# A fused attention and feed-forward kernel on one core: context sums copied whole and put together by DMA, a batch's last contexts in the next one's first step, row statistics and weight loads in pieces

## The reference

```python
x = x + _layernorm(attention(_layernorm(x), Wq, bq, Wk, bk, Wv, bv, Wo, bo))   # 32 heads of 16
x = x + _layernorm(ffn(_layernorm(x), gate_w, up_w, down_w, scales))           # 512 -> 1536 -> 512
# attention: softmax(q k^T / 4) v per head; ffn: down(silu(gate(x)) * up(x)),
# where each weight is first rounded to float8 (e4m3) and widened again
```

## Time and profile before

| | us |
|---|---|
| median of three runs (lowest, highest) | 1712.83 (1712.39, 1716.59) |
| the profiled execution's own time | 1714.72 |
| its span, first to last instruction | 1712.9 |
| PE busy | 1585.2 (93%) |
| DVE busy | 1191.8 (70%) |
| ACT busy | 908.0 (53%) |
| POOL busy | 619.7 (36%) |

### The profile page before, as it was taken

The page is one execution under the profiler, slowest core; times in us unless marked ns, Lnnn a source line. Parts: engine busy times, 40 slices in busy tenths (PEclk is TensorE's granted clock), DMA queues, the critical chain, the costliest instruction groups (busy, mean ns, idle before and its releaser), DMA issues.

```text
span 1712.9 us, 22893 instructions
## 1 busy us (share of the span) xinstructions
PE 1585.2 (93%) x8266; PEld 728.8 (43%) x8266; DVE 1191.8 (70%) x2200; ACT 908.0 (53%) x1624; POOL 619.7 (36%) x504
## 2 busy tenths in 40 slices
PE   4899999999999999999999999879999999999996
PEld 3433333333334334333333433215555555555553
DVE  6698898898888888888888888764254353353433
ACT  3177676666766767767767766672222222222221
POOL 4124343533633542542443352143332232232331
PEclk9799999999999999999999999979999999999998
DMA  3412212312211312321221121510201201201110
GB/s 115 102 37 72 52 45 71 88 50 65 79 56 50 97 35 60 91 55 51 84 73 49 46 81 41 164 56 19 87 25 50 74 25 49 75 25 50 50 50 25
DMA packets 81740, 105.63 MB, mean 62 GB/s; under 512 B 16214, under 2 KB 46934, under 8 KB 81624
## 3 DMA queue, kind: packets, MB, share of 16 engines
q1 hardware_dynamic: 81628, 104.17, 20.8%
HBM read 52.71 MB, written 21.50 MB: 43 GB/s over the span
## 4 chain that ended last, share of the span: by engine, by line
PE 61%; DVE 24%; ACT 8%; issue 5%; DMA 1%; POOL 1%; SPq 1%; POOLq 0%; ACTq 0%; DVEq 0%
PE ring L1371 19%; PE side L1001 13%; DVE maxima L832 11%; PE down_sums L1385 10%; PE contexts L1076 8%; PE scores L1063 6%; PE maxima_scores L1040 4%; ACT probs L741 3%; DVE channel_shift_bits L971 2%; DVE channel_shift_bits L969 1%; DVE denominators L857 1%; DVE qkT L816 1%; DVE stats_in L787 1%; DVE y L823 1%; DVE ctx_raw L862 1%
## 5 line engine op out<-in xcount | busy, mean ns | idle before, releaser
L832 DVE TENSOR_REDUCE maxima<-maxima_scores 128x1 f32<-128x512 f32 x1024 | 655.5, 679 | 92.7 <-PE maxima_scores L1040 87.4
L741 ACT ACTIVATE probs<-scores 128x512 f32<-128x512 f32 x1024 | 549.4, 601 | 283.8 <-PE scores L1063 283.1
L1040 PE MATMUL maxima_scores<-k_stack,q_stack 64*128 64x512 f16 x1024 | 340.2, 390 | 47.2 <-DVE maxima L832 46.7
L1063 PE MATMUL scores<-q_stack,k_stack 64*128 64x512 f16 x1024 | 326.8, 390 | 14.2 <-ACT probs L741 8.1
L1076 PE MATMUL contexts<-probs,v_around_ones 128*32 128x512 f32 x2048 | 278.7, 616 | 8.4 <-ACT denominators L685 3.5
L1321 DVE SCALAR_TENSOR_TENSOR fuse<-ring,up_scale,gate 128x512 f32<-128x512 f32 x96 | 72.0, 750 | 292.9 <-PE ring L1371 284.2
L1235 POOL TENSOR_TENSOR fuse_low<-fuse,fuse_high 128x512 fp32r<-128x512 f32 x96 | 137.8, 1436 | 372.7 <-ACT fuse_high L1257 372.7
L1257 ACT CAST fuse_high<-fuse 128x512 fp32r<-128x512 f32 x96 | 59.4, 619 | 291.9 <-PE down_sums L1385 270.0
L1063 PEld LDWEIGHTS scores<-q_stack,k_stack 64*128 64x128 f16 x1024 | 65.5, 94 | 339.6 <-ACT probs L741 183.2
L1385 PE MATMUL down_sums<-down_q,fuse_high 128*128 128x512 f32 x384 | 168.0, 437 | 1.1 <-issue 0.8
L1371 PE MATMUL ring<-xT_high_ffn,gate_q 128*128 128x512 f16 x384 | 146.6, 382 | 7.4 <-DVE xT_low_ffn L1294 5.9
(11 more groups left out here) (201 smaller groups left out, 2409.4 us busy)
## 6 DMA issues: line engine op xcount, KB each, us to landing
q_stack<-qkT SPq DMA_DIRECT2D x192, 64.0 KB, 2.0
k_stack<-qkT SPq DMA_DIRECT2D x192, 64.0 KB, 2.0
x_rows<-in_L_attn_hidden_states SPq DMA_DIRECT2D x8, 1024.0 KB, 5.3
x_residual<-in_L_attn_hidden_states SPq DMA_DIRECT2D x32, 256.0 KB, 2.9
middle_rows<-y SPq DMA_DIRECT2D x32, 256.0 KB, 3.3
x_rows_ffn<-middle_rows SPq DMA_DIRECT2D x8, 1024.0 KB, 5.6
x_residual_ffn<-middle_rows SPq DMA_DIRECT2D x8, 1024.0 KB, 7.9
out_rows<-y_ffn SPq DMA_DIRECT2D x32, 256.0 KB, 2.2
```

The source lines that it names most:

```text
L741: act.activation(probs[:, n % 2, j, :], work[(b * (GH * STEPS) + GH * n + j) % RING][:], ACT.Exp, scale=float(D) ** -0.5).then_inc(p_full, 1)
L832: dve.tensor_reduce(maxima[:, g % 2, at:at + 1], bank[:], AX.X, ALU.max).then_inc(rot_free, 1)
L1040: mm = pe.matmul(bank[:], q_st[half, s, qc * P:qc * P + P], k_st[half, s, :], start=True, stop=True)
L1063: mm = pe.matmul(work[i % RING][:], k_st[half, s, c * P:c * P + P], q_st[half, s, :], start=True, stop=True)
```

## The change

- **Context sums.** ACT copies the bank whole: after the even group to `ctx_raw` (one operation for two), after the odd group to a new tile `ctx_odd_groups`. DVE's two masked additions and its shuffle are gone. SP puts the halves together with DMAs of 16 partitions by 512: four for the even denominators (`denominators_even`, at n = 5, 13, 21, 29), and four for the odd denominators and four for the odd contexts (`contexts_together`, at n = 9, 17, 25 and at n = 1 of the next batch). ACT's `invert` now waits for those DMAs, POOL's `normalise` too.
- **Seam.** `contexts(b, 31)` moves from the end of the batch into step 0 of the next, between score 1 and score 2.
- **Order within steps.** ACT's `invert` stands inside the step, its logarithm behind exponential 1, its exponential behind exponential 3 (steps 2, 10, 20, 26), and `refine` behind exponential 1 of the step after. POOL's last reciprocal and `normalise` of a batch move from steps 1 and 2 of the next to 2 and 3. The transposes of the next batch's rows move from the end of steps 12 to 15 to the head of steps 13 to 16. The weight jobs move to other steps. `aggregate` is cut in two (three sums, then four more operations) in steps 3 and 4, 18 and 19; statistics of the next batch's rows are in steps 0 and 2 and no longer in 1 and 2. ACT's normalisation of the output rows is in steps 20 to 23.
- **FFN weights.** The last batch loads the scales at n = 14, gate and up weights in four pieces each at n = 15 to 22, the down weights in four pieces at n = 23 to 26; DVE widens three blocks each at the end of steps 28 to 31.

```diff
...
@@ -250,3 +259,3 @@
     MAXIMA = NH * T
-    XT0 = 12
+    XT0 = 13
@@ -273,3 +282,3 @@
         if XT0 <= n < XT0 + T and b < B - 1:
-            out.append((("x", n - XT0), b + 1))
+            out.insert(0, (("x", n - XT0), b + 1))
         if n >= STEPS - T and b == B - 1:
@@ -335,3 +344,3 @@
     MAGIC_AT, SUM_AT, BIG_AT, ROUND_AT, STORE_AT = (
-        (2, 7, 12, 22, 27), (3, 8, 13, 23, 28), (4, 9, 14, 24, 29), (5, 11, 15, 25, 30), (6, 12, 16, 26, 31))
+        (6, 10, 14, 20, 26), (7, 11, 15, 23, 29), (8, 12, 16, 24, 30), (9, 13, 18, 25, 31), (10, 14, 19, 26, 31))
     gate_w, up_w, down_w = ffn_weights
...
@@ -433,2 +443,22 @@
+        def denominators_even(k):
+            slot = k % O % 2
+            sp.wait_ge(c0_out, k + 1)
+            if k > 1:
+                sp.wait_ge(c_l, k - 1)
+            for j in range(GH):
+                lo = 2 * D * j
+                sp.dma_start(den[lo:lo + D, slot, :], ctx_raw[lo + D:lo + 2 * D, slot, :]).then_inc(den_even, 16)
+
+        def contexts_together(k):
+            slot = k % O % 2
+            sp.wait_ge(c1_out, k + 1)
+            for j in range(GH):
+                lo = 2 * D * j
+                sp.dma_start(den[lo + D:lo + 2 * D, slot, :], ctx_odd[lo:lo + D, :]).then_inc(den_odd, 16)
+            sp.wait_ge(den_even, (k + 1) * GH * 16)
+            for j in range(GH):
+                lo = 2 * D * j
+                sp.dma_start(ctx_raw[lo + D:lo + 2 * D, slot, :], ctx_odd[lo + D:lo + 2 * D, :]).then_inc(ctx_in, 16)
+
         fill(0, 0)
...
@@ -490,3 +522,10 @@
                     sp.dma_start(ffn.ds_rows[:], down_s.partition_broadcast(P)).then_inc(ffn.s_in, 16)
-                    sp.dma_start(ffn.down_in[:], down_d.rearrange("(f p) h -> p f h", p=P)).then_inc(ffn.w_in["down"], 16)
+                if last and 15 <= n < 15 + 2 * KC:
+                    name, c = ("gate", "up")[(n - 15) // KC], (n - 15) % KC
+                    rows, dst = ((gate_d, ffn.gate_q), (up_d, ffn.up_q))[(n - 15) // KC]
+                    sp.dma_start(dst[:, c, :], rows[c * P:c * P + P, :]).then_inc(ffn.w_in[name], 16)
+                if last and 23 <= n < 23 + DOWN_PARTS:
+                    part = ffn.F // DOWN_PARTS
+                    blocks = slice((n - 23) * part, (n - 23) * part + part)
+                    sp.dma_start(ffn.down_in[:, blocks, :], down_d.rearrange("(f p) h -> p f h", p=P)[:, blocks, :]).then_inc(ffn.w_in["down"], 16)
                 if n == 18 and b + 2 < B:
...
@@ -586,5 +627,5 @@
             for n in range(STEPS):
-                if n == 1 and b:
-                    times_reciprocal(b * O - 1, O - 1)
                 if n == 2 and b:
+                    times_reciprocal(b * O - 1, O - 1)
+                if n == 3 and b:
                     normalise(b * O - 1, O - 1, None)
...
@@ -683,4 +724,10 @@
                 act.wait_ge(c_l, b * O + o - 1)
-            act.mul(ctx_raw[:, o % 2, :], cps[:], half_mask[:, 0:1]).then_inc(c0_out, 1)
-            act.mul(den[:, o % 2, :], cps[:], half_mask[:, 1:2]).then_inc(c0_out, 1)
+            act.copy(ctx_raw[:, o % 2, :], cps[:]).then_inc(c0_out, 1)
+
+        def contexts_odd(k):
+            act.wait_ge(pv_done, PV0 + (2 * k + 2) * T)
+            if k > 0:
+                act.wait_ge(ctx_in, k * GH * 16)
+                act.wait_ge(den_odd, k * GH * 16)
+            act.copy(ctx_odd[:], cps[:]).then_inc(c1_out, 1)
@@ -688,7 +735,9 @@
-            act.wait_ge(den_sh, k + 1)
+            act.wait_ge(den_even, (k + 1) * GH * 16)
+            act.wait_ge(den_odd, (k + 1) * GH * 16)
             if k > 0:
                 act.wait_ge(c_l, k)
-
             act.activation(rec[:], den[:, o % 2, :], ACT.Ln).then_inc(den_ln, 1)
+
+        def invert_back(k):
             act.wait_ge(den_ln, k + 1)
...
@@ -725,14 +773,8 @@
                 before = side_end(b, n - 1)
+                if XT0 <= n < XT0 + T and not last:
+                    turned_high(b + 1, n - XT0)
                 if before:
                     side_high(before[1], before[0], side_at[before])
-                if n == 1 and b:
-                    invert(b * O - 1, O - 1)
-                if n == 2 and b:
-                    refine(b * O - 1, O - 1)
-                if n in (10, 20, 26):
-                    o = (10, 20, 26).index(n)
-                    invert(b * O + o, o)
-                if n in (11, 21, 28 if last else 27):
-                    o = n // 8 - 1
-                    refine(b * O + o, o)
+                inverted = {2: b * O - 1, 10: b * O, 20: b * O + 1, 26: b * O + 2}.get(n, -1)
+                refined = {3: b * O - 1, 11: b * O, 21: b * O + 1, 28 if last else 27: b * O + 2}.get(n, -1)
                 act.wait_ge(pv_done, PV0 + b * STEPS + n - 1)
@@ -741,10 +783,16 @@
                     act.activation(probs[:, n % 2, j, :], work[(b * (GH * STEPS) + GH * n + j) % RING][:], ACT.Exp, scale=float(D) ** -0.5).then_inc(p_full, 1)
+                    if j == 1 and inverted >= 0:
+                        invert(inverted, inverted % O)
+                    if j == 1 and refined >= 0:
+                        refine(refined, refined % O)
+                    if j == 3 and inverted >= 0:
+                        invert_back(inverted)
+                if n % 8 == 0 and b * O + n // 8:
+                    contexts_odd(b * O + n // 8 - 1)
                 if n % 8 == 4:
                     contexts_even(b, n // 8)
-                if XT0 <= n < XT0 + T and not last:
-                    turned_high(b + 1, n - XT0)
                 if n in (6, 7, 8, 9) and not last:
                     normalise("in", x_rows, xn_ready, b + 1, n - 6)
-                if n in (18, 19, 21, 22) and b:
-                    normalise("out", y, yn_ready, b - 1, (18, 19, 21, 22).index(n))
+                if 20 <= n < 20 + T and b:
+                    normalise("out", y, yn_ready, b - 1, n - 20)
                 j = job_at(BIG_AT, b, n)
...
@@ -852,17 +901,2 @@
-        def denominators_odd(b, o):
-            k = b * O + o
-            dve.wait_ge(pv_done, PV0 + b * STEPS + (2 * o + 2) * T)
-            dve.wait_ge(c0_out, (k + 1) * 2)
-            dve.scalar_tensor_tensor(den[:, o % 2, :], cps[:], half_mask[:, 0:1], den[:, o % 2, :], ALU.mult, ALU.add).then_inc(c1_out, 1)
-
-        def contexts_odd(b, o):
-            k = b * O + o
-            dve.wait_ge(c1_out, ODD0 + k * 2 + 1)
-            dve.scalar_tensor_tensor(ctx_raw[:, o % 2, :], cps[:], half_mask[:, 1:2], ctx_raw[:, o % 2, :], ALU.mult, ALU.add).then_inc(c1_out, 1)
-
-
-        def shuffle(o):
-            dve.stream_shuffle(den[:, o % 2, :], den[:, o % 2, :], [(i + D) % 32 for i in range(32)]).then_inc(den_sh, 1)
-
         def channel_factors():
@@ -932,6 +966,2 @@
                     first_rows()
-                if last and n == 24:
-                    dve.wait_ge(ffn.w_in["down"], 16)
-                    for f in range(ffn.F):
-                        dve.tensor_copy(ffn.down_q[:, f, :], ffn.down_in[:, f, :]).then_inc(ffn.down_ready, 1)
                 if last and n == 27:
@@ -941,4 +971,8 @@
                                           ffn.norms["in"]["rstd"][:, t:t + 1], ALU.subtract, ALU.mult).then_inc(ffn.xn_ready, 1)
-                for k, (item, of) in enumerate(items):
+                k = -1
+                for item, of in items:
                     reduce_maxima(of, item)
+                    if item[0] == "x":
+                        continue
+                    k += 1
                     if k == 0 and before:
...
@@ -953,12 +987,11 @@
                         stats("in", x_rows, t)
-                    if n == 3 and k == 1 and not last:
-                        moments("in", b + 1)
-                    if n == 18 and k == 1 and b:
-                        moments("out", b - 1)
-                    if n % 8 == 0 and n and k == 1:
-                        denominators_odd(b, n // 8 - 1)
-                    if n % 8 == 0 and n and k == 2:
-                        contexts_odd(b, n // 8 - 1)
-                    if n % 8 == 1 and n > 1 and k == 0:
-                        shuffle(n // 8 - 1)
+                    if n in (3, 4) and k == 1 and not last:
+                        moments("in", b + 1, ((sums, spreads)[n - 3],))
+                    if n in (18, 19) and k == 1 and b:
+                        moments("out", b - 1, ((sums, spreads)[n - 18],))
+                if last and n >= STEPS - DOWN_PARTS:
+                    part, i = ffn.F // DOWN_PARTS, n - STEPS + DOWN_PARTS
+                    dve.wait_ge(ffn.w_in["down"], DOWN_PARTS * 16)
+                    for f in range(i * part, (i + 1) * part):
+                        dve.tensor_copy(ffn.down_q[:, f, :], ffn.down_in[:, f, :]).then_inc(ffn.down_ready, 1)
                 j = job_at(MAGIC_AT, b, n)
...
@@ -1123,2 +1156,5 @@
                 what, i, lo, hi, later = side_step(b, n)
+                if items and items[0][0][0] == "x":
+                    rot_item(items[0][1], items[0][0])
```

(5 more changed lines are left out.)

## The result

The changed kernel takes 1630.34 us (three runs, 1627.21 to 1630.97) against 1712.83: a ratio of 0.9507, 95% interval [0.9479, 0.9535]. In a later comparison it took 1627.9 us, ratio 0.9499 [0.9486, 0.9512]. Forecast were 1634 us and a range of 1606 to 1672. The profiled execution has a span of 1629.0 us against 1712.9: 83.9 less, of which the six middle batches give 70.3 (136.73 to 125.02 in the mean), the first 7.9, the last 11.5; the tail behind the last contexts takes 5.6 more, the start 0.2.

The account below looks back on a forecast made before the run. PE bounds the kernel at 3.67 us a step and DVE interrupts it. Six middle batches -67, first batch -5, last -9, tail +2.2 sum to -78.8 us: 1712.8 to 1634 us, range 1606 to 1672.

Parts of the forecast that it names:

- Seam: Step 31 and the next step 0: PE no longer stands until ACT has made step 31's four exponentials, 10.3 to 7.5, -2.8 us.
- Context sums: DVE and ACT lose operations per pair; counted beyond the seam only in steps 8 to 11, 16.5 to 15.5, -1.0 us.
- 1 and 2: Steps 1 and 2 of a middle batch, now without a weight job: 8.5 to 7.5, -1.0 us.
- 17 to 20: Steps 17 to 20, where aggregate's seven operations, the shuffle and the inversion are taken apart: 16.95 to 15.1, -1.8 us.
- 26 to 28: Steps 26 to 28, where the weight job at n = 27 no longer falls in POOL's normalise: 12.4 to 11.3, -1.1 us.
- 22 and 23: Steps 22 and 23, where the weight job at n = 22 no longer falls in POOL's normalise: 8.7 to 7.4, -1.3 us.
- Steps 3 to 5: Up to three DVE waits for POOL's normalise in step 4 (L65, L67 above 1 us), or by another reading one: -1.2 us.
- 12 to 16: Row transposes ahead of their step: 22.9 to 21.4, -1.5 us; step 13 stays near 4.95 because of ACT's load.
- Step 21: ACT has four operations, 2.75 us, between steps 20 and 21, so score 3 waits: 4.4 to 4.95, +0.55 us.
- New DMAs: 48 per batch on SP, 0.59 us an issue, landing 2.0 us after, all hidden: 0 us.
- Last batch: Maxima wait 4.85 to about 3, down weights moved -8, late denominators and maxima in steps 25 to 28 +5: together -9 us.
- Tail: Behind the last contexts: an ACT copy (0.6), four issues and a landing (1.8 + 2.0) replace 2.2 us: +2.2 us.

Follow-up runs that it names:

- jobs_before: The changed kernel with the weight jobs back in the steps they had before the change: 1650.82 us, ratio 0.9633.
- third_pair_later: The changed kernel with the third pair's inversion in step 27 and its refinement and normalise in step 28, one step later each: 1623.51 us, ratio 0.9462.
- moments_at_6: The changed kernel with all seven statistics operations for the next batch's rows in step 6, ACT's row normalisation in 7, 8, 9 and 11: 1623.69 us, ratio 0.9463.
- jobs_clear: The changed kernel with the weight jobs of steps 10 and 14 moved to 11 and 16: 1630.0 us, ratio 0.9501.
- dmas_halved: The changed kernel with each of the 12 new DMAs of a pair issued as two of half the columns, same bytes: 1711.37 us, ratio 0.9974.
- best_three: The changed kernel with row statistics in step 6, third inversion in step 27 and step 10's weight job one step later: 1615.47 us, ratio 0.9424.

## Why the prediction was right

The forecast missed by 4 us of 82, in part by luck: the six middle batches, the first and the last gave 3.3, 2.9 and 2.5 us more than forecast, the tail 3.4 less. Its account (PE the bound, DVE's lag the loss) held; how it shared out the gain did not, and it left out the clock. Each step by its own terms:

- *The bound* (PE at 3.67 us a step, DVE interrupting it): right. Twenty of 32 steps now run at 3.66 to 3.77, and every edit that took a DVE or ACT delay away brought its steps to just that.
- *Seam*, -2.8: the size was right (-2.98; -3.13 if the seam before is measured to 621.16, where the score of step 1 starts, and not to 621.01), the cause was not. The forecast had PE stand until the four exponentials of step 31 were made; in the trace before, contexts 31 (614.36) follow the last projection matmul without a gap, and PE stands behind them, for DVE's maxima. Seam and steps 1 and 2 together fell from 18.80 to 14.75. Of these 4.05 us, the place of the contexts gives 0.7 back when it is undone, the masked additions 1.5, the weight job nothing. Of the 1.8 that are left, up to 1.6 is the estimate for the stretch at the low clock, which comes back with neither.
- *Context sums*, -1.0: mis-sized. Undone by themselves they cost 5.3 us a batch, most of it through DVE. Their share was booked under 1 and 2, 17 to 20 and 26 to 28, whose sums were right but of which the named causes explain only part. The places' sums held since they came from the windows; the shares, from reasoning, did not. The weight jobs are worth 2.9. With 0.6 for the transposes and 0.7 for the contexts that is 9.5 of 11.7. Most of the other 2.2 may be the clock; the rest belongs to edits that were not undone by themselves (the inversion between exponentials, `aggregate` in halves, POOL a step later) or to their meeting.
- *1 and 2*: -1.07 against -1.0, for another cause than the one named: with the weight job back in step 2 they still take 7.43 (jobs_before). *17 to 20, 22 and 23*: -2.0, -1.4 against -1.8, -1.3; the old places of the jobs bring back only 0.6 of the 1.4. *26 to 28*: -0.96 against -1.1; in step 27 the late denominators take 0.5 of it back in batch 3 (third_pair_later).
- *First batch*: -7.9 against -5; no run was made for it.
- *Steps 3 to 5*: -1.57 against -1.2. The mechanism is shown (moments_at_6). Of the two readings that the forecast set against each other, three waits and one, neither came: two were full and one lasted 0.2 us. L65 took 1.27 as the forecast's sign had it, L67 only 0.17.
- *12 to 16*: -0.83 against -1.5. Step 13 is 4.87, as forecast (4.95), but ACT's load is not why (jobs_clear). The transposes are worth 0.8 in these steps. What holds steps 13 to 15 stays open; in step 13 DVE stands 1.54 us for ACT's half of a row transpose, in 14 and 15 some 0.5, and this was not tried by itself.
- *Step 21*, +0.55: wrong in sign, -0.16. ACT's four operations from 529.04 are followed by the exponential at 531.31: 2.27 us, not the 2.81 that their durations add up to (2.75 in the forecast), since each starts some 0.1 us before the one ahead of it ends. That is 0.5 of the 0.7 us by which the term is off. ACT:

```profile
529.04 0.65 ACT L744 ACTIVATE reciprocals<-reciprocals 128x512 f32<-128x512 f32 x1
529.56 0.60 ACT L725 COPY ctx_raw<-contexts 128x512 f32<-128x512 f32 x1
530.02 0.85 ACT L718 ACTIVATE y<-y,offset_out,rstd_out 128x512 f32<-128x512 f32 x1
530.74 0.71 ACT L709 ACTIVATE qkT<-side,bias_qk 128x512 f16<-128x512 f32 x1
531.31 1.12 ACT L783 ACTIVATE probs<-scores 128x512 f32<-128x512 f32 x2
```

- *New DMAs*, 0: right in price (0.589 against 0.59) and almost in cover in the middle batches; they cost 0.6 a batch through the third inversion. At twice the price nearly all of the gain would be gone (dmas_halved).
- *Last batch*, -11.5 against -9: step 24 gave 3.1 as expected; the wait for the maxima in step 19 fell from 4.85 to 4.18 only, against 3 forecast; the late denominators made step 27 6.2 us long (3.3 before; PE waits 3.1 in it), and its neighbours gained more. PE's mean clock in this batch rose from 0.89 to 0.93; how much of the 11.5 that is was not separated.
- *Tail*, +5.6 against +2.2 (4.3 in the second profile of the same kernel). The chain was right: copy 0.58, four issues, landing; the logarithm starts 5.3 us behind the contexts, where it was 2.3 before. But the issues took 3.24 us, where the forecast's 0.59 each would give 2.4, and while ACT waited, PE ran out of work, for 4.3 us, and came back at the low level of its clock, a mean of 0.71 in the stretch where before it had 1.00:

```profile
1072.00:1082.40 10.40, 6.07 (x18) 2.17 (x17) 1.50 (x2) 5.79 (x8) 8.67 (x7) 0.71 0.52 158
```

The term left out what a longer wait does to the clock; so did the seam's.

## What to carry to other kernels

Work that is taken off an engine with little slack is worth time in every step that it had made late, not only where it stood: price it by the lag that it hands on (here 8 us less work on DVE was most of 5.3 us a batch). A window can hold the price of a wait elsewhere: steps 1 and 2 were full of busy PE and slow, since the clock had fallen behind the seam; read the clock column before a loss is given to what stands in the window. Two small linked operations in another engine's chain of long ones cost a whole operation of that chain each; moving them some steps, behind the chain, gave 1.0 us a batch for nothing. And a wait of PE can cost twice, by its own length and by the lower clock behind it (tail: PE idle 4.3 us, mean clock 0.71; seams before: 1.7 us idle, then 3.41 us at half the clock).

## What was not expected of the hardware

- Two queues that issue small DMAs at the same time took 0.98 us an issue each. One queue alone took 0.84 at the same place (four in 3.37 us, best_three), against a median of 0.59 over all: two queues saved 1.4 us of 3.4.
- An issue of one kind can hold SP much longer than usual: `q_stack<-zeros` 2.38 us in batch 4, 0.53 in batch 1.
- Behind each of seven seams in which PE stood 1.7 us, its clock was at the low level for 3.41 us.
- A DVE operation of 4 columns that is held ends 0.02 us after the POOL operation that it waits for (L56, L65), one of 512 columns 0.28 us after it (L1004, step 10): almost all of the held time is the wait.
- Operations of ACT that follow each other without a gap overlap in the records: 2.81 us of durations in 2.27 us (step 20 to 21).
